# Expert products in smaller pieces, and a new order of all lanes, in a one-core kernel of three interleaved lanes

## What is computed

```python
x = x + 0.5 * ffn0(ln(x))      # weights and inputs quantized in blocks of 16
x = x + mamba(ln(x))           # 2 layers, 256 channels x 16 states, a scan over the tokens
x = x + 0.5 * ffn0(ln(x))
x = x + 0.5 * moe(ln(x))       # 8 experts, every token through all of them
x = x + attention(ln(x))       # 16 heads of 8 features, causal
x = x + 0.5 * moe(ln(x))

# moe: h = relu(x @ W1[e] + b1[e])   (128 -> 512 features)
#      out += gate[:, e] * (h @ W2[e] + b2[e])   (512 -> 128)
```

## Time and profile before

| | |
|---|---|
| Median of 3 runs | 2767.91 us (2762.08 to 2769.0) |
| The profiled execution's own time | 2769.06 us |
| Its span, first to last instruction | 2767.3 us |
| Mean granted clock of PE | 0.955 of full speed |
| Busy: PE, DVE, ACT, POOL | 94%, 70%, 58%, 50% |
| Expert pass 1, first and last item | 403.3 and 508.5 us |
| Expert pass 2, first item | 645.0 us |
| Last item of lane a on PE | 2344.5 us |
| Last expert pass (alone on PE), first item | 2691.5 us |

### The profile page before, as it was taken

One profiled execution on the slowest core, in us unless ns is written; L12 is line 12 of the kernel. 1 busy time (PEld: TensorE's weight loads), 2 busy tenths in 40 slices (PEclk: granted clock), 3 DMA queues, 4 the chain that ended last, 5 costly groups with the idle time before them and its releaser, 6 DMA issues.

```text
span 2767.3 us, 41433 instructions
## 1 busy us (share of the span) xinstructions
PE 2610.0 (94%) x14847; PEld 1899.4 (69%) x14847; DVE 1942.1 (70%) x3753; ACT 1605.7 (58%) x3405; POOL 1375.6 (50%) x1227
## 2 busy tenths in 40 slices
PE   7999999998999889999899898989999999998998
PEld 7878875786687555776477566756676677667675
DVE  5979888797969786867849887788859766332310
ACT  1433437535665647756476566747675775565654
POOL 1458475573838364735617483574627536211011
PEclk9999999999999999999779899999999989999999
DMA  4223122231213120202102120211202122000000
GB/s 153 67 67 113 54 69 78 61 92 39 86 38 100 46 71 29 85 24 70 61 20 89 39 84 20 66 58 47 81 17 77 35 62 62 1 5 1 1 5 4
DMA packets 88572, 150.58 MB, mean 54 GB/s; under 512 B 10565, under 2 KB 21485, under 8 KB 88110
## 3 DMA queue, kind: packets, MB, share of 16 engines
q1 hardware_dynamic: 88366, 147.94, 17.6%
HBM read 145.26 MB, written 2.65 MB: 53 GB/s over the span
## 4 chain that ended last, share of the span: by engine, by line
PE 73%; DVE 12%; ACT 6%; issue 5%; POOL 4%; DMA 0%; POOLq 0%; SPq 0%; DVEq 0%; ACTq 0%
PE c_bank L913 15%; PE c_bank L921 15%; PE c_bank L1340 8%; PE a_bank L759 6%; PE b_bank L1073 3%; DVE hst L707 3%; PE b_bank L1062 3%; PE a_bank L749 3%; PE b_bank L1086 2%; PE b_bank L1085 2%; PE a_bank L728 2%; DVE a_bank L701 2%; POOL prod_c L830 1%; PE b_bank L581 1%; PE b_bank L1084 1%
## 5 line engine op out<-in xcount | busy, mean ns | idle before, releaser
L830 POOL TENSOR_TENSOR prod_c<-hst,prod_c 128x512 f32<-128x512 f32 x512 | 664.5, 1305 | 426.5 <-DVE hst L707 399.7
L707 DVE TENSOR_TENSOR_SCAN hst<-dA,a_bank 128x512 f32<-128x512 f32 x512 | 620.7, 1212 | 10.4 <-ACT dA L819 2.6
L819 ACT ACTIVATE dA<-delta,a_neg 128x510 f32<-128x510 f32 x512 | 365.3, 719 | 349.2 <-DVE hst L707 344.6
L913 PE MATMUL c_bank<-c_xT,w 128*128 128x512 f32 x1024 | 539.8, 631 | 13.7 <-ACT weighted_y L956 8.3
L921 PEld LDWEIGHTS c_bank<-w,hid 128*128 128x128 f32 x4096 | 494.5, 193 | 68.2 <-issue 31.3
L921 PE MATMUL c_bank<-w,hid 128*128 128x128 f32 x4096 | 517.5, 279 | 0.2
L1340 PEld LDWEIGHTS c_bank<-ident 128*128 128x128 f32 x3686 | 454.6, 194 | 46.5 <-issue 37.1
L1340 PE MATMUL c_bank<-ident 128*128 128x128 f32 x3686 | 463.8, 278 | 0.2 <-ACT weighted_y L956 0.2
L972 POOL TENSOR_TENSOR xs<-xs,weighted_y 128x512 f32<-128x512 f32 x128 | 169.4, 1323 | 556.5 <-ACT weighted_y L956 556.4
L948 ACT ACTIVATE hid<-c_bank,b 128x512 f32<-128x512 f32 x512 | 349.1, 687 | 148.6 <-PE c_bank L913 146.9
L701 DVE TENSOR_TENSOR a_bank<-du,a_bank 128x512 f32<-128x512 f32 x512 | 348.2, 680 | 46.5 <-PE a_bank L749 44.7
(11 more groups left out here) (180 smaller groups left out, 3573.1 us busy)
## 6 DMA issues: line engine op xcount, KB each, us to landing
prod_c<-c_rows SPq DMA_DIRECT2D x512, 256.0 KB, 3.2
w<-in_w SPq DMA_DIRECT2D x2, 2048.0 KB
xs<-in_x SPq DMA_DIRECT2D x8, 256.0 KB, 9.2
bias<-skew SPq DMA_DIRECT2D x1, 2048.0 KB, 8.2
out_dram<-xs SPq DMA_DIRECT2D x8, 256.0 KB, 2.3
in_wT<-in_in_wT SPq DMA_DIRECT2D x1, 512.0 KB
c_rows<-bcC SPq DMA_DIRECT2D x16, 32.0 KB, 1.6
b_hq<-in_w_gu SPq DMA_DIRECT2D x1, 384.0 KB, 3.1
```

Of the source, the lines that this page charges most:

```text
L707: nc.vector.tensor_tensor_scan(hst[:, s % RS, :], dA[:, s % RA, :], b_bank, 0.0, ALU.mult, ALU.add).then_inc(M.h.sem, 1)
L819: nc.scalar.activation(half_batches(dA[:, s % RA, :], 1), half_batches(delta[:, h, :], 1), ACT.Exp, scale=a_neg[:, l, h, n:n + 1]).then_in ...
L830: nc.gpsimd.tensor_tensor(prod[:, s % RP, :], hst[:, s % RS, :], cring[:, s % RC, :], ALU.mult).then_inc(M.pp.sem, 1)
L913: nc.tensor.matmul(S.bank[up_bank(e, c)][:, :], w1[:, e, c * 128:(c + 1) * 128], S.xT[:, :], start=True, stop=True).then_inc(M.up.sem, 1)
```

## The change

Two things are changed in `moe_pe`. Each up product is issued as two products of 256 tokens into the two halves of the same bank, with a `yield` between them; the wait stands ahead of the first, the semaphore rises with the second. Each down product of four chunks has a `yield` after its second chunk; its instructions are the same. And all five order strings are new.

```diff
@@ -910,7 +915,11 @@ moe_pe
-                        nc.tensor.matmul(S.bank[up_bank(e, c)][:, :], w1[:, e, c * 128:(c + 1) * 128], S.xT[:, :],
+                        half = TOK // 2
+                        nc.tensor.matmul(S.bank[up_bank(e, c)][:, 0:half], w1[:, e, c * 128:(c + 1) * 128], S.xT[:, 0:half],
+                                         start=True, stop=True)
+                        yield
+                        nc.tensor.matmul(S.bank[up_bank(e, c)][:, half:TOK], w1[:, e, c * 128:(c + 1) * 128], S.xT[:, half:TOK],
                                          start=True, stop=True).then_inc(M.up.sem, 1)
                         yield
...
                             ins = nc.tensor.matmul(S.bank[down_bank(f)][:, t * D:(t + 1) * D],
                                                    hid[:, f % 2, j, t * 128:(t + 1) * 128], w2[:, f, j, :],
                                                    start=(j == 0), stop=(j == HC - 1))
+                            if j == 1:
+                                yield
...
 ORDER_SP = (
-    "a249c2a59caca83ca54ca49ca33c3")
+    "a241caca52caca68ca66ca66ca33c3")
```

More of the change, by code:

```diff
@@ new lines @@
+    "adbd3ad2ad15ad8ad5ca2cacbc5ac4ac4b2c4b2c4b2c6ac4ac4bc3b3c5ac4ac12ac4ac3b5cbc8ac4a2c2ac2bcb2c3b2c4b2c4ac12a2"
+    "c4bc2ac3b3c13a4d14ad8a2cacb6a4cac3a3c3aca2c2ac4a2c2ac5a2c5ac2aba2c3b2caba2bc4bc3a2c4acba2c6abac3ac6acb2c7ac7"
+    "abc3bc3b2c2bc2b3c2b3c2b6c2b6acb3ab3ab3ab2c2abc3b3ab6ab3ab3acb3c5bcb5ac2b3ab3c2b3acb3c2b2cbc2b2cba2b3ac2b6a2"
+    "b3ab2a2c2b2ab2cba3c5acbabac2ac3a2d3ad8a3c2acabc5ac4ac4bc4bc10bc4bc12bc4bc12b2c4bc12a2c4ac12abc4ac2b2c10ac4b"
+    "c18ab2a2bad9a2d7ad10ad9a2d13ad17ad15abcb2cb2acbaba2c3bab3c3ac2a2c3ac4b5cacbac8ac9a2c2ac2bcacb2caba2bc4bac3b"
@@ new lines @@
+ORDER_ACT = (
+    "abab24a13ba3baba5ba10b3a2b2a8b2ab2a83b4a8baba5ba4ba8b5a12bab2aba5b3aba7b2c4bcbca4ca5b5a3c3a3c2a3ca2ca2ca6b2"
+    "c3ab2c2ac3a2c4ac2acaca2c3ac2ac2aca2c4ac2ac2a3c5ac3a3c5a2c2aca2c4ac4a8b4a8baba5ba4ba8b5a12bab2aba5b3aba7b2c4b"
+    "cbca4ca4b2ab3a3c3a3c2a3ca2ca2ca6b2c3ab2c2ac4ac4ac2aca2cbab3ac4ac2acab4abc4ab3acb2c2baca2c4b2ac2bcac5ab2ac2bc"
+    "acac2ac2ac4a3b29a4ba4b4a4b3ab3ab3ab3a4b3a3b3a2ba2ba6b3abab3ab3a2b3a2b3a2b3a2b3a2b3a2b3a2b3a2b3ab3a2b3ab2a2b"
+    "a2b2ab2c2ac5bc4a4c2ba4c2b2c5ac2acb5c5ac2aca2c5ac2a3cb2ab2c5abab3aca6c2abab2c5bc3ac6ab2c2ab3c8a2c4aca2cb2ab2c"
+    "a2cab2ab2cacac2acac2a2c3b2ab2c2abcab3acb2cba2c5acb2ac2bc5b2c2bc6b2cb2cb3cbababa2b2a2ba2b3a3b3ab3c4b3ab3ab3a"
+    "b3a2cbab2ab3c2b2aba2b3ab2abab2aba2b5aba3b3cb3ab3acb3c4b3cb3cab3cab6ab3ab3ab4aba2cac3ba2c4ab4a2c4ac2acabac4a"
+    "c2bc7bc8bc8b3c10acac5b2cac2b2ac16b2a4b4c4ba4cba4cbacba3cb2a2bab2ca3ca2ca2ca2cb2a2b2a2cacac3b4c5ab4abab3a2c4"
+    "b2c2bcb2abcac4b2cbcac2ac5acab2c2b2ab3ab3ab3ab3acb3cac3b3acb3ab3cab3cab3ab3ab3ab3ab3acb3ac3b3c2b5cbcb15a4baba"
+    "ba2b3c2a3bab3ab2c2a2b3ab2abab3acbc3a2ba5ba6b4ac4ac2ababcabac4ac3bacac5ab2cacb3aca2c6ac2ac5acab2ab2cac6b4a2c3"
+    "a2c5ac3ababac2ac3bc2bc9b2a4bcb2c2a4caca3b2ab2aca6ba2ba6b2ca2cb4c2bcab2abc2b2abc2b2abac5b3cac2a2c6ac2a3cb2c3a"
+    "cacb2cacab3a2b3c3b3cab3cab3cab2cbab3acb3ab3ab3a2b6c4b6cb3cb3cb6ca4ba4b5a4c2b2abcb2acacab3ca3bc2b2a3b3a2ba2ba"
+    "b2ab3abab2ab3acab3c3babc2ac2ba2b4ac5ac2aba2bcacbacac2ac2bacac5ac3a2b2c3bab2c5a2c5ac2acac3b2acb2ac3acb4ac15bc"
+    "ba4ba5ba3c8ab2a2bc3b2ca3ca4ca2b2a2b2a3cac4b4c2acacab4cac3bac2b3acab2cb4c4acb2cbc5ab2c2ab2cb3cab3cab6ab3ab3a"
+    "b3ab6ab3ab6c2b3cac2b3ab3ab3cab4cb2acab3ab6ac4b3acbcb3cb2cb6c4b3cb2cbcb3ca3b3a4bac3bca4bc4a4c4a3c2b4a2ca3ca2c"
+    "acac2a2c2a2cabac7abca3c4acac2baca2c3ac2ac2aca2c4bac3acac5ab2cb3cacacac5ac2ac4ab2ab2ac2ac2b8cbc3b3cb5ca4bca4"
+    "b3a4cbcbcbcbab3a2cbcb2a3b2a2ca2ba2b2cba2b3c4ab3cb2cbacb3a2cb6a2b3ac4b3cab2cbacb3cab3ac4b3a2cb3cacb3ca2b3ab3"
+    "c4acb3cab3cacb3ab3ac4b2cbab3c2b3ab3ca2b3c4ab3cbacbcacba2c19bcbcbcbc14bc2bc6bc3bc7b2cbc5b2c3b4c8b4c4b4c4b4c4"
+    "b3cb2cb2cb2c5bcbcb2cb6c2b3c3b3c2b3cb8cbc3b3cb6cb3cb3cb6c4b3c2b2cbcb6c2b2c2bcbcb2cb3cb3c5b3c2b3cb6c2b3c3b3c2"
+    "b3cb2c4bc8b4c2b4cb4cb3c2b3c2b3c3b4c4b3c2b3c2b6c4b6cb6cb6cb6cb6c2b3c3b3c2b3cb3c4b3c2b3c2b8c2bc2b2cbcb2cbcb2cb"
+    "c4b3c2b3cb6c3bcbc2bc73")
@@ new lines @@
+ORDER_POOL = (
+    "ab5a2b2a13ba86bababa18ba11ba16baca2b2aca7ca6ca6ca9ca6ca6ca3ca6bababa18ba11ba16baca2b2aca3ca4ba3ca3ba3ba3ca8c"
+    "a3ca6ca3ca51bca6ba3cbc2b2cba3cabca3c2aca3ba8ba10ba3ca3ba6ca5ca2ca3ca3ca13ca3cbaca5ba6c2bc2ba3ca2cac2a4ba7cba"
+    "b2aba2cba2ba5ca3ca4ca11ca15ca8c2baca2ba10bca8ca3bca6bca6caba5ca6cbc2ab2ababa8ca5ca6ca9ca16ca5caca3ca2bca4b"
+    "a15cba4ca4ca2ba2ca3ba5ca3cbacbc2ba2ba3babaca6ca3ca15ca11ca6ca3c3b2a3ca6ca8ca6ca3baca7ca3bca5bca3bca2ba2ca7c"
+    "a7ca8ca8ca6ca7ca3c2a3bcbc2bc2bcb2cbc11b3c17")
```

122 lines of the change are left out of this document (48 added, 74 removed).

## The result

The changed kernel took 2775.16 us, the median of 20 runs (2770.64 to 2784.38), beside 2763.13 us for the kernel before in 20 runs (2759.69 to 2771.32). The ratio is 1.0041, with an interval of 1.0030 to 1.0051: it is slower by 0.4%, some 12 us. The time lies inside the range; the direction was wrong.

The account below looks back on a forecast made before the run. PE's issue was taken to bound the kernel, with POOL level in front. 2769.1 + 3 (halves) + 8 (front placeholders) + 0 + 0 - 27 (finer pieces) = 2753.1, forecast 2752 us after median adjustment; range 2708 to 2803.

Parts of the forecast that it names:

- What bounds the kernel: Whole kernel: PE's issue sets the time, busy 94%; between 32 and 415 us PE and POOL run neck and neck.
- The up products' halves: Expert up products on PE: 1024 more passes and loads, loads hidden; 0 to 4 us, taken as 3.
- loads stand bare: Rival, up halves' weight loads on PE: 1024 unhidden loads at 0.112 us, 115 us more, 2868 us; chance 0.03.
- The front's placeholders: Ahead of the second expert pass: 175 more, 39.1 us, mostly covered by POOL's pace and PE's idle time; 8 us.
- The middle's placeholders: Second expert pass to lane a's end: 152 more, 33.9 us, taken by idle time and slow clock; 0, bounds 0 and 34.
- placeholders set the pace: Rival, PE in front and middle: the room does not take the added placeholders; put at 2795 us, chance 0.32.
- The finer pieces: From 790 us on: other lanes' ready items wait 0.215 us less behind 493 expert items; 27 us gained of at most 106.
- the relu comes later: from 0 up to the gain, cancelled: ACT's relu after the up product's second half: items between halves delay it and what queues behind; no cost taken.
- the down products' yield: 0: Down products on PE: the yield adds no instruction and no wait, 0 us.
- The other strings, 0: Orders of SP, DVE and ACT: same items in another order, SP's wait of some 7 us hidden; 0 us.
- The check named for the gain: Second expert pass to lane a's end: idle time and clock loss down 27 us or more, lane a's last item near 2330.
- the gain is hidden anyway: Rival: lanes wait for the scan and each other, or the later relu takes the gain back; 2768 us, chance 0.18.

Follow-up runs that it names:

- the kernel with 175 fewer: Changed kernel without 175 of its PE placeholders, all ahead of the second expert pass: 2761.56 against 2761.35 us for the kernel before, 1.0004.
- the pieces apart: The changed kernel itself, its order letting other lanes' items stand between an expert product's two pieces in 307 of 1024 cases: 1.0041 to the kernel before.
- whole products at the first place: Changed kernel's order and placeholders, each expert product issued uncut where its first piece stood: 2764.61 against 2765.63 us for the kernel before, 1.0001.
- placements with whole up products: Four kernels in the changed kernel's order, up product uncut; up, down at first, first 1.0001; second, apart 1.0023; first, apart 1.0050; second, second 1.0070.
- Whole products at the second place: Changed kernel's order and placeholders, each expert product issued uncut where its second piece stood: 2787.38 us, 1.0070 to the kernel before.
- the kernel with both repairs: Changed kernel with uncut expert products where their first pieces stood and 175 fewer placeholders ahead of the second expert pass: 2753.37 against 2764.43 us, 0.9964.
- The table of placements: Ratios to the kernel before, in the changed kernel's order; rows place the down product, columns the up product: first piece's place, cut, second piece's place; 1.0001 to 1.0070.
- up at the second place: Changed kernel's order, up products uncut where their second half stood, down products still in two items: 1.0023 to the kernel before.
- up at the first: Changed kernel's order, up products uncut where their first half stood, down products still in two items: 1.0050 to the kernel before.
- down first and up apart: Changed kernel's order, down products uncut where their first piece stood, up products still in halves: 1.0016 to the kernel before.

## Why the prediction was wrong, by its own steps

**What bounds the kernel** held: PE sets the time, and in the front PE and POOL run neck and neck. The chain of the kernel after:

```profile
239.85 0.86 PE a_bank L764 x2
240.71 0.22 PE a_bank L754
240.93 1.56 PE c_bank L1351 x14
242.49 0.22 PE a_bank L754
242.71 0.89 PE c_bank L1351 x8
243.60 0.86 PE a_bank L764 x2
```

A pair with 11 placeholders (22 passes) takes 3.75 us, as worked out, with nothing in it but PE. POOL's starts in the same layer still stand 3.80 us apart:

```profile
243.14 2.50 POOL L835 TENSOR_TENSOR prod_c<-hst,prod_c 128x512 f32<-128x512 f32 x2
246.94 2.49 POOL L835 TENSOR_TENSOR prod_c<-hst,prod_c 128x512 f32<-128x512 f32 x2
```

**The up products' halves, +3.** Right as far as it can be told: about 2 us, and at most 5, by the kernel that has them and nothing else new. The timeline, passes of line 919 and 922 in a row:

```profile
427.53 0.59 PE L922 MATMUL c_bank<-c_xT,w 128*128 128x256 f32 x2
427.96 0.59 PE L919 MATMUL c_bank<-c_xT,w 128*128 128x256 f32 x2
428.39 0.59 PE L922 MATMUL c_bank<-c_xT,w 128*128 128x256 f32 x2
```

Two passes take 0.43 us, 0.215 each. The last expert pass, alone on PE, took 75.9 us, from its first item at 2706.59 to the end, against 75.8 us before. The loads are hidden, and the rival "loads stand bare" falls. The Trainium skill's row-group rule ("TensorE: Matmul & The Clock Gate", section "The mechanism"), read by its first half alone, would have given that rival; the trace does not agree, by the 0.215 us.

**The front's placeholders, +8 (0 to 39).** Right in place and size: +10.3 us at the second pass, and 10 us come back without them. The room within the loops was nearly as counted: from the first scan of a layer to its last the kernel after takes 0.9, 0.9, 0.9, 0.0 and 0.8 us longer than the kernel with 175 fewer, 3.5 us in the front's five layers. The greater part of the 10 us lies ahead of the loops and between them (the first scan of all starts at 99.77 against 97.71 us), where the 15 us of PE's idle time had been counted as cover.

**The middle's placeholders, 0 (0 to 34).** Wrong in its bounds, and on the safe side: in the new order their price is below zero, as taking them out cost 14 us. The end below nothing was not considered. Without them PE is idle for 11 us more and runs at half speed for longer, by the clocks above. The rival *placeholders set the pace* is right in the front, for 10 us. In the middle of the new order, where it needed its 26 to 34 us, it is refuted; in the old order's middle it would have held, with 36.5 us.

**The finer pieces, -27 (0 to 106).** This is the step that failed, and with it "the relu comes later: from 0 up to the gain, cancelled" and "the down products' yield: 0". The step saw half of the exchange. Another lane's item that comes in between the pieces starts up to 0.43 us earlier, but the expert product is complete later by all that stands in between, and its consumer waits for that. I did name this for the relu, where no cost stands clear of the intervals, and cancelled it against the gain. For the down product I priced only the instruction. There the gate scaling waits 35 us more (222.1 against 186.6). In place of -27 the pieces apart measured +11 us against whole products at the first place (1.0041 against 1.0001), of which some 2 are the halves' passes. And the time does not lie in waits of PE: across the placements with whole up products its idle time is the same, and what grew is its time at half speed, for which the sum had no term.

The row on which I leaned for the gain did shrink, and it was still not the pieces'. PE's loads waited 67.3 us for the scan before. In the kernel after, and with whole products at the first place, it reads:

```profile
PEld a_bank L754 <- DVE hst L712: 19.7, 26, 2.7
```

```profile
PEld a_bank L750 <- DVE hst L708: 29.5, 47, 2.7
```

Whole products at the second place have 27.2 us. So the new order takes away most of these waits with whole products too. The halves without the new order leave 59.2 us of them.

**The other strings, 0.** With whole products at the first place and the front's placeholders gone the new order is 11 us faster than before, though its middle still has 152 placeholders more. That is a gain of some 40% of the size that I gave to the pieces, and it comes without them. How it divides between PE's, DVE's and ACT's strings was not tried.

**The named checks.** The first item of the second pass, POOL's starts, the halves' distance, the last pass and the stretch behind lane a (418.2 us) came as forecast. The check named for the gain, idle time and the clock's loss together down by 27 us or more, was fulfilled without its other half, lane a's last item near 2330: from 855 to 2345 us PE's idle time went from 89 to 72 us and the clock's loss from 90 to 73, 34 us together, and the placeholders grew by the same 34 us there (60.5 to 94.3). So nothing was left over for the time, and the check didn't tell the pieces from the placeholders. Lane a's last item at 2364.3 us was past the 2355 named for the placeholders' rival; the kernel with the same middle and 175 fewer in front has it at 2343.8, so front and clock put it there.

**The sum** of what the runs show: new order -10, front's placeholders +10, the pieces with their distance +11, together +11 against 12 measured. The rival *the gain is hidden anyway* comes nearest by its second half, "the later relu takes it back", with the down product in the relu's place. It allowed 8 us to either side of the kernel before; the 12 us measured lie outside, as the pieces took back more than they gave.

**What stays open.** The table of placements does not order along its middle row: up at the second place (1.0023) reads lower than up at the first (1.0050), with intervals that just overlap and scaling waits that are alike (223.8 and 221.3 us). Their clocks differ as their times do (0.969 and 0.966), and two of the seven runs of the slower one took 2771 to 2772 us, as the faster one's do, the other five 2780 to 2785. That reads as a stretch at half speed that comes in some runs and not in others; it is not shown for the other placements. That the later down product acts through the scaling's wait is argued from the agreement of wait and time over the rows of that table. No run removed the wait itself, and what leads from it to PE's lower clock is open. POOL's add behind the scaling gives no link: it waits 525.8 us with whole products at the first place and 544.2 in the kernel after, but 542.0 with down first and up apart.

## What to carry to other kernels

Cutting an item in two lets others in between, and delays its completion by all that is let in: price both, for each consumer, before crediting the cut, and try the whole item at its first piece's place, which keeps the new order without the delay. Count filler work by place and by order: in the front it cost a quarter of its length, in the middle of the new order it was worth 14 us because PE would have stood idle and slowed, and in the middle of the old order it cost all its length. When the busy work is the same and the idle time too, look at the granted clock: here it held the whole difference between four placements. When a new order brings both a cut and a reshuffle, the comparison that isolates the cut depends on where the uncut item is put; two such places gave opposite signs here.

## What the runs showed of the hardware

The times of one program fall in groups 10 to 15 us apart. The kernel with both repairs ran at 2751 to 2756 us with a mean granted clock of 0.971 to 0.973, or at 2766 to 2767 us with 0.967 to 0.968, on the same chip. The kernel after ran at 2771 to 2778 us and four times at 2784. One place where profiles differ in this way is around 1150 us. Windows of PE alone (length, busy, granted clock, then the DMA columns), the kernel after, profiled in its higher group, and the one with 175 fewer in front, profiled in its lower; their middles are the same:

```profile
1100.00:1130.00 30.00, 30.00 (x194) 1.00 0.01 2
1130.00:1145.00 15.00, 15.00 (x64) 0.54 0.23 72
1145.00:1160.00 15.00, 14.04 (x73) 0.69 0.13 36
1160.00:1175.00 15.00, 15.00 (x50) 0.52 0.05 17
```

```profile
1100.00:1130.00 30.00, 30.00 (x148) 0.84 0.13 37
1130.00:1145.00 15.00, 14.23 (x96) 0.87 0.07 25
1145.00:1160.00 15.00, 15.00 (x100) 1.00 0.24 61
1160.00:1175.00 15.00, 15.00 (x111) 1.00 0.37 110
```

PE is busy nearly throughout in both, but in the first it runs for some 40 us near its lower level, 1.2 GHz. One minus the clock, times the length, summed: 18.8 us held back, against 6.8 us in the second. These 12 us are as much as the whole effect under study. The loss stays: the scans of the two kernels are 10.1 us apart at 1147 us of the kernel after and 21.3 at 1185, and lane a's last items 20.5. The kernel with both repairs, profiled at 2766.7 us, has 0.50 and 0.75 in the third and fourth window. Ahead of the fall at 1130 us PE had no idle time, 30.00 of 30 us; 77 of its 194 instructions there are the attention's products of 9 columns. Idle time alone doesn't tell, then, where the clock falls. And a single profile is no measure of an edit of 10 us; here the ratios of many runs decide, and the profile shows where to look.
